# Undivided exponentials, parameter loads on another queue, an earlier end of the first half, and split operands for every second layer

## The reference

```python
# x (512, 64, 768), H = 4 heads, E = 8 experts, HD = 384
scores  = where(x.sum(-1) != 0, x @ aw, -inf)            # (512, 64)
feature = einsum('bl,bld->bd', softmax(scores), x)       # (512, 768)
g       = softmax(relu(feature @ gW1[h] + gb1[h]) @ gW2[h] + gb2[h])   # per head h
gate    = g[row, D[row]]                                 # (512, 8)
h1 = relu(BN1(feature @ eW1[e] + eb1[e]))                # per expert: (512, 768)
h2 = relu(BN2(h1 @ eW2[e] + eb2[e]))                     # per expert: (512, 384)
rep = einsum('be,ebo->bo', gate, h2)
out = softmax((rep @ hW[h] + hb[h])[row, D[row]])        # (512, 2)
```

## Time and profile before

| | |
|---|---|
| median of 3 runs (lowest, highest) | 595.87 us (595.14, 596.85) |
| the profiled execution | 595.4 us, span 593.6 us |
| PE busy | 514.3 us (87%) |
| DVE busy | 482.8 us (81%) |
| ACT busy | 454.4 us (77%) |
| moved | 168.05 MB, mean 283 GB/s |

### The profile page before, as it was taken

How to read it: one execution, slowest core, us unless ns; L and a number is a source line. 1 busy time by engine, 2 the same in 40 slices (tenths; PEclk the granted TensorE clock), 3 DMA queues, 4 the chain that set the end, 5 groups by cost and what they waited for, 6 DMA issues and landing times.

```text
span 593.6 us, 11283 instructions
## 1 busy us (share of the span) xinstructions
PE 514.3 (87%) x4191; PEld 416.1 (70%) x4191; DVE 482.8 (81%) x961; ACT 454.4 (77%) x1007; POOL 81.2 (14%) x118
## 2 busy tenths in 40 slices
PE   0456576666899999999999999899999999999995
PEld 0111121211878888878888888789999999999995
DVE  6989999998799898888999999765376767566753
ACT  5989999997699989888899899564555655565651
POOL 0000000001022030211212121111222222222200
PEclk9976777867799999999999999999999999999998
DMA  8999999999999999999889973545555665666520
GB/s 314 400 367 402 400 401 402 385 367 362 402 396 397 381 394 390 381 382 354 311 311 341 362 277 121 161 137 180 168 160 163 192 182 179 181 184 195 164 77 0
DMA packets 52339, 168.05 MB, mean 283 GB/s; under 512 B 4797, under 2 KB 5041, under 8 KB 52285
## 3 DMA queue, kind: packets, MB, share of 16 engines
q1 hardware_dynamic: 36012, 100.88, 44.6%
q0 software_dynamic: 16128, 66.07, 33.9%
q10 hardware_dynamic: 144, 0.39, 0.2%
HBM read 167.32 MB, written 0.00 MB: 282 GB/s over the span
## 4 chain that ended last, share of the span: by engine, by line
PE 56%; DVE 22%; DMA 11%; issue 7%; ACT 2%; SPq 1%; ACTq 0%; DVEq 0%
PE z_ps L880 15%; PE z_ps L881 15%; PE z_ps L882 15%; DVE prod_out L631 14%; DMA xring<-in_r_x_dram 11%; PE feat_ps L942 5%; DVE wlo L619 4%; PE z_ps L911 4%; ACT copy_out L434 1%; DVE h_hi L687 1%; DVE h L707 1%; PE turn_ps L975 0%; SPq L360 0%; DVE score L631 0%; ACT whi L419 0%
## 5 line engine op out<-in xcount | busy, mean ns | idle before, releaser
L631 DVE CUSTOM_DVE_ANT_0 prod_out<-xring,aw_bc 128x768 bf16<-128x768 f32 x256 | 233.3, 946 | 6.9 <-DMA xring<-in_r_x_dram 6.3
L434 ACT ACTIVATE copy_out<-xring 128x768 bf16<-128x768 f32 x256 | 212.6, 832 | 9.9 <-DMA xring<-in_r_x_dram 8.9
L880 PE MATMUL z_ps<-feat_hi,whi 128*128 128x256 f32 x720 | 207.5, 288 | 2.5 <-DVE feat_lo L666 1.2
L881 PE MATMUL z_ps<-feat_lo,whi 128*128 128x256 f32 x720 | 204.6, 284 | 0.0
L882 PE MATMUL z_ps<-feat_hi,wlo 128*128 128x256 f32 x720 | 204.5, 284 | 0.0
L619 DVE TENSOR_TENSOR wlo<-wraw,whi 128x1152 fp32r<-128x1152 f32 x106 | 143.4, 1353 | 69.8 <-ACT whi L419 69.2
L419 ACT ACTIVATE whi<-wraw 128x1152 fp32r<-128x1152 f32 x106 | 122.8, 1159 | 56.5 <-PE z_ps L882 56.4
L880 PEld LDWEIGHTS z_ps<-feat_hi,whi 128*128 128x128 f32 x720 | 139.2, 193 | 4.0 <-DVE feat_lo L666 1.6
L881 PEld LDWEIGHTS z_ps<-feat_lo,whi 128*128 128x128 f32 x720 | 139.0, 193 | 0.0
L882 PEld LDWEIGHTS z_ps<-feat_hi,wlo 128*128 128x128 f32 x720 | 138.9, 193 | 0.0
L942 PE MATMUL feat_ps<-xring,pwin 128*32 128x384 f32 x1024 | 114.6, 586 | 19.2 <-ACT pwin L452 19.2
(11 more groups left out here) (102 smaller groups left out, 333.8 us busy)
## 6 DMA issues: line engine op xcount, KB each, us to landing
xring<-in_r_x_dram SPq DMA_DIRECT2D x128, 768.0 KB, 8.1
wraw<-in_L_rec_eW_dram POOLq DMA_DIRECT2D x90, 576.0 KB, 4.5
wraw<-in_L_rec_gW_dram POOLq DMA_DIRECT2D x16, 576.0 KB, 4.5
w2raw<-in_L_rec_eW_dram POOLq DMA_DIRECT2D x6, 576.0 KB, 7.4
aw_bc<-in_L_rec_aw_dram ACTq DMA_DIRECT2D x1, 384.0 KB, 5.5
w2raw<-in_L_rec_gW_dram SPq DMA_DIRECT2D x1, 48.0 KB
h<-in_L_rec_eb_dram SPq DMA_DIRECT2D x1, 24.0 KB
h<-in_L_rec_bn_g_dram SPq DMA_DIRECT2D x1, 24.0 KB
```

What stands on the lines that cost most here:

```text
L434: nc.scalar.activation(copy_out[:, t % 2, :], xring[:, r % RING_ROUNDS, j, i, :], ACT.Copy, accum_out=rowsum[:, r % 2, t:t + 1]).then_inc( ...
L631: nc.vector.tensor_tensor_reduce(out=prod_out[:, t % 2, :], in0=xring[:, r % RING_ROUNDS, j, i, :], in1=aw_bc[:, :], scale=1.0, scalar=0.0 ...
L880: nc.tensor.matmul(psum_tile, w_hi, a_hi, start=first, stop=False)
L881: nc.tensor.matmul(psum_tile, w_hi, a_lo, start=False, stop=False)
```

## The change

- The exponentials stay undivided. Four more elements stand behind each row of `xring`, the first of them a one, so the second half of `feat_ps` gets a 385th column, the sum of the exponentials of each row. `copy_rows` takes its reciprocal once per block (`norm`) and scales the rows with it. `softmax_norm` and the sums of `softmax_exp` go. Rows of `xring` are now 772 elements apart and not 768.
- The twelve parameter loads are issued by POOL, after the second score tile, and not by SP.
- At the end of the first half: in the last round ACT takes `softmax_exp` and `place_probs` of the round before earlier, DVE takes `softmax_max` ahead of the parameters, `copy_rows(1)` stands ahead of the tiles of round 16, of which two move behind `features_lo(1)`, and unit 0 waits for the first half of the split features only.
- `NATIVE = 0`: the second layers of experts 0 to 2 of the first half are split like all others, and the panels stand in the order a, c of the expert before, b from the start.
- The stationary operand that picks an expert's gate is read as a broadcast of `sel` and no longer copied by DVE (`pick_gate` goes).

```diff
-NATIVE = 3
+NATIVE = 0
...
-        xring = sb("xring", [P, RING_ROUNDS, CG, 2, DM])
+        xring = sb("xring", [P, RING_ROUNDS, CG, 2, DM + 4])
+        x_in = xring[:, :, :, :, 0:DM]
...
-            for r in range(RING_ROUNDS, ROUNDS):
+            for r in range(ROUNDS):
                 load_round(r)
...
+            pool.wait_ge(zeroed, 1)
+            pool.wait_ge(scored, 2)
...
+                pool.dma_start(prm_rows[at:at + src.shape[0], a, :], src).then_inc(prm_loaded, 16)
...
             for r in range(FIRST_ROUNDS):
-                sum_rows(r, range(0, 4))
+
+                at = 3 if r == FIRST_ROUNDS - 1 else 4
+                sum_rows(r, range(0, at))
                 if r:
                     softmax_exp(r - 1)
-                sum_rows(r, range(4, 5))
+                sum_rows(r, range(at, at + 1))
+                if r:
+                    place_probs(r - 1)
+                sum_rows(r, range(at + 1, at + 2))
                 if r == BLOCK_ROUNDS + 1:
                     copy_rows(0)
-                sum_rows(r, range(5, 7))
-                if r:
-                    place_probs(r - 1)
-                sum_rows(r, range(7, ROUND_TILES))
+                sum_rows(r, range(at + 2, ROUND_TILES))
...
             def copy_rows(b):
                 dve.wait_ge(feat_added, (b + 1) * BLOCK_ROUNDS)
-                nc.vector.tensor_copy(rows[:, DM // 2:DM], feat_ps[:, 1, 0:DM // 2]).then_inc(rows_b, 1)
+                if b:
+                    dve.wait_ge(rows_a, b)
+                nc.vector.reciprocal(norm[:, :], feat_ps[:, 1, DM // 2:DM // 2 + 1]).then_inc(norm_ready, 1)
+                dve.wait_ge(norm_ready, b + 1)
+                nc.vector.tensor_scalar(rows[:, DM // 2:DM], feat_ps[:, 1, 0:DM // 2], norm[:, :], None,
+                                        ALU.mult).then_inc(rows_b, 1)
...
-                if third == 2 and FIRST_ROUNDS < r <= ROUNDS:
-                    softmax_norm(r - 1)
...
-                if s in (gate_at(c) for c in range(NCH)):
-
-                    pe.wait_ge(feat_ready, 2 * CB * (UNITS[s][0] + 1))
+                for c in range(NCH):
+
+                    if s - gate_at(c) in (0, 1):
+                        pe.wait_ge(feat_ready, 2 * CB * (c + 1) - 1 + s - gate_at(c))
                 unit(s)
```

More of the change, by code:

```diff
@@ L133, in rec_kernel @@
         ADD_SLOT = {unit_of(c, "c", q, 1) + 2: (c, q) for c in range(NCH) for q in range(E) if (c, q) != (NCH - 1, E - 1)}
-        PICK_SLOT = {unit_of(c, "c", q, 0): (c, q) for c in range(NCH) for q in range(E)}
+        GATE_SLOT = {unit_of(c, "c", q, 1): (c, q) for c in range(NCH) for q in range(E)}
         def gate_at(c):
@@ L196, in rec_kernel @@
         head_is = sb("head_is", [P, NBLK, H])
-        sel = sb("sel", [P, E])
-        pick = sb("pick", [P, P], F32R)
+        sel = sb("sel", [P, E], F32R)
         gl = sb("gl", [P, CB, E])
@@ L349, in load_round @@
                     b, rb = divmod(r, BLOCK_ROUNDS)
-                    sp.dma_start(xring[:, r % RING_ROUNDS, j, :, :],
+                    sp.dma_start(x_in[:, r % RING_ROUNDS, j, :, :],
                                  x_v[b, rb, :, j, :, :]).then_inc(x_loaded[r % RING_ROUNDS][j], 16)
[L353 to L366, removed]
-            for r in range(RING_ROUNDS, ROUNDS):
+            for r in range(ROUNDS):
                 load_round(r)
@@ L433, in sum_rows @@
                         act.wait_ge(mask_ready, r - 1)
-                    nc.scalar.activation(copy_out[:, t % 2, :], xring[:, r % RING_ROUNDS, j, i, :], ACT.Copy,
+                    nc.scalar.activation(copy_out[:, t % 2, :], x_in[:, r % RING_ROUNDS, j, i, :], ACT.Copy,
                                          accum_out=rowsum[:, r % 2, t:t + 1]).then_inc(summed, 1)
@@ L455, in copy_rows @@
             def copy_rows(b):
-                act.wait_ge(feat_added, (b + 1) * BLOCK_ROUNDS)
-                nc.scalar.activation(rows[:, 0:DM // 2], feat_ps[:, 0, 0:DM // 2], ACT.Copy).then_inc(rows_a, 1)
+                act.wait_ge(norm_ready, b + 1)
+                nc.scalar.activation(rows[:, 0:DM // 2], feat_ps[:, 0, 0:DM // 2], ACT.Copy,
+                                     scale=norm[:, :]).then_inc(rows_a, 1)
             def features_hi(b, g):
@@ L808, in _ @@
                     mask_scores(r - 1)
-                score_tiles(r, range(1, 3))
+                score_tiles(r, range(1, 2))
                 if r:
                     softmax_max(r - 1)
+                score_tiles(r, range(2, 3))
                 if r == BLOCK_ROUNDS + 2:
@@ L936, in add_features @@
                 for i in range(2):
-                    if i and between is not None:
-                        turn_scores(between)
                     at = WIN - (4 * in_block + 2 * i)
                     for half in range(2):
+                        if between is not None and (i, half) == turn_at:
+                            turn_scores(between)
                         for j in range(CG):
-                            last = nc.tensor.matmul(feat_ps[32 * j:32 * j + 32, half, 0:DM // 2],
+                            last = nc.tensor.matmul(feat_ps[32 * j:32 * j + 32, half, 0:DM // 2 + half],
                                                     pwin[:, 2 * j + i, at:at + 32],
-                                                    xring[:, r % RING_ROUNDS, j, i, DM // 2 * half:DM // 2 * (half + 1)],
+                                                    xring[:, r % RING_ROUNDS, j, i,
+                                                          DM // 2 * half:DM // 2 * (half + 1) + half],
                                                     start=(in_block == 0 and i == 0),
@@ L965, in gate_broadcast @@
                     pe.wait_ge(gated_ready, n)
-                nc.tensor.matmul(gate_bc, pick[:, :], gateT[:, :], start=True, stop=True).then_inc(gate_bc_ready, 1)
+                nc.tensor.matmul(gate_bc, sel[:, q:q + 1].to_broadcast([P, P]), gateT[:, :], start=True, stop=True).then_inc(gate_bc_ready, 1)
             def gate_logits(c):
```

68 lines of the change are left out of this document (31 added, 37 removed).

## The result

The changed kernel takes 588.87 us (median of 4 runs, 588.21 to 589.30) against 595.5 before (a fourth run beside the three of the table ahead): ratio 0.9886, 95% interval 0.9864 to 0.9908. Forecast were 589.2 us and "faster". Its profiled execution took 588.99 us, its span is 587.2.

A forecast was written before the change was run, and what follows sets the result against it. It took the stream of x to bound the first half, DVE beside PE the split slots. First-half gains of 5.6 us and the panels' effect gave 6.2 in all: 595.4 - 6.2 = 589.2 us, own range 586.5 to 592.

The forecast's parts named there:

- What bounds it: The stream of x paces the first half, DVE nearly as much as PE the split slots, PE alone the end.
- PE waits for `wlo` or `h1` in slots 20 to 50: A sign in the second half that would show the forecast right: PE waiting there for these DVE outputs.
- (a): First half, parameter loads moved off SP: the gap in the stream of x closes, 0.7 us, bounds 0 and 1.4.
- (b): First half, no division on DVE: it is some 0.2 us behind at the last load, not 1.4; gain 1.2 us.
- (c): Last round of the first half, probabilities placed earlier: mask to products 4.3 us, not 5.4; gain 1.1, bounds 0 and 2.4.
- (d): End of the first half, from round 15's products to the first unit: 2.9 us after them, not 5.5; gain 2.6.
- part 1: The first half: four gains sum to 5.6 us, first unit at about 146.1, bounds 148.8 and 143.4.
- Full DMA takes 1.4 of it: Round 16's last loads come through a full DMA, so DVE starts 4.2 us earlier, not 5.6.
- Part 2: Unsplit panels and second half: PE alone gains 5.5 us, DVE gets net 9.4 more; total gain 4.9 to 8.5, taken 6.2.
- DVE keeps up: Rival: DVE's idle time shrinks further or it starts as early as PE; gain 11.1, 584.3 us; chance 0.13.
- DVE takes nearly all: Rival: about 9 us of DVE's idle time stay, PE gains only some 2.4 us, 593.0 us; chance 0.20.
- The longer pitch: Rival: rows of x 3,088 bytes apart slow the stream; at 5% the time is 598.5 us; chance 0.08.

The follow-up runs named there:

- experiment 10: Changed kernel with the gating of experts 3, 4 and 5 of the first half cut to 2 of 256 columns: 587.03 us, one run.
- experiment 5: Changed kernel with the twelve parameter loads back in SP's queue between rounds 3 and 4: 589.82 us.
- experiment 0: The changed kernel run again, unedited, as the measure for the others: 588.68 us.
- Experiment 6: Changed kernel with the scores of round 9 turned after the first quarter of the products, not the third: 588.79 us.
- Experiment 4: Changed kernel with copy_rows(1) behind the three tiles of round 16 again and unit 0 waiting for both halves of the split features: 591.11 us.
- experiment 2: Kernel before the change with only NATIVE = 0, so all panels split and divisions kept: 598.94 us.
- experiment 1: Changed kernel with NATIVE = 3, the second layers of experts 0 to 2 kept in fp32: 587.40 us.
- 7b: Changed kernel with NATIVE = 1, one panel left unsplit: 587.47 us.

## Why the prediction was right, step by step

The forecast 589.2 us lies 0.3 us from the measured 588.9. What bounds the kernel was right; that the sum came so near is in part luck, as its parts were off both ways.

- **What bounds it**: right. DVE's busy time (209.6; 209.5 forecast), its idle rest (3.9 us; 4.3 forecast) and the length of its stretch came as worked out, and experiment 10 shows directly, for units 29 to 51, that DVE sets the pace. The way it does so was not foreseen: the sign "PE waits for `wlo` or `h1` in slots 20 to 50" did not come. All of PE's 5.5 us of waits between 170 and 375 us are for ACT's `h`, and ACT stands at DVE's maxima for 9.7.
- **(a)** 0.7: some 0.5 (experiment 5).
- **(b)** is the step that failed: "Without it DVE is faster than the stream and no longer 136.23 - 134.86 = 1.4 us behind at the last load, but some 0.2". Counted from the landing of that load, DVE was 1.7 us behind before the change and 1.4 after it (135.43 against 134.04), 1.9 in experiment 0. An edit that the list of the change leaves out turns the scores of the next round after the third quarter of the products and not after the second; I had not followed it through round 10. There DVE stood 2.3 us and was 3.6 behind in round 11, and it regains only 0.35 to 0.55 us a round. Experiment 6 undid this alone, and the lag was gone, but the time stayed: these 1.2 us were not worth anything at the end.
- **(c)** 1.1, or 2.4 if the clock is up: mask to products took 2.9 us (137.19 to 140.09) instead of 5.4, a gain of 2.5, with the clock up. In experiment 0, at the lower clock, it was 1.0.
- **(d)** 2.6: 5.8 us (140.09 to 145.86) instead of 8.3, a gain of 2.6; 2.2 in experiment 0. Experiment 4 puts 2.4 us on the whole time.
- **The sum of part 1** was 5.6 and came as 5.8 in the profiled pair, with (b) nearly at nothing and (c) at its bound. That is luck of the executions: in experiment 0 the same code gives 3.2, and over all traces with either code the first unit is 1.8 to 5.9 us earlier. From the bounds that the prediction gives for (a) and (c) follow 147.9 and 144.1 for the first unit, not 148.8 and 143.4.
- **Full DMA takes 1.4 of it**: 1.6 of the lead was gone at unit 6, but not by the loads alone. Left out was the gain of the first units at the higher clock (2.0 us by unit 2, where the prediction had up to 2.3); PE then lost 3.7 us, most of it to its waits for ACT and to the lower clock behind them. A DVE start 4.2 us earlier was forecast; the first tile of round 17 was 5.0 earlier.
- **Part 2**: the gain "between 4.9 and 8.5" was 6.4 at unit 51 in experiment 0 (6.5 in the first profile), where I took 6.2. DVE handed on 6.0. That it hands on only what it starts earlier is not borne out: in experiment 0 it starts 1.8 us later than in the first profile and ends its stretch only 0.1 later, with 2.6 us idle instead of 3.9. What the parts are worth I had not seen either. PE's 3.4 us on panels, which stand in "PE alone would gain 5.5", are no gain by themselves: alone the split is a loss of 3.8 (experiment 2), here of 1.6 from unit 6 to 51. The division, which I counted as relief of DVE and a stall of 2.06, is worth 3.8 where panels stay unsplit and 7.5 where they don't. For these executions 4.2 from the first half, 3.8 from the division, less 1.6 for the split make the 6.4.
- **Rivals**: *DVE keeps up* fell here; with two panels unsplit and one wait less it is nearly so, 585.8. *DVE takes nearly all* fell as DVE began earlier and kept 3.9 us idle, not 9. *The longer pitch* fell: 402 GB/s.

Two things stay open. Between executions of the same code the start of unit 6 differs by up to 3.7 us; in the first profile and in experiment 1 a lower clock between 162 and 170 us (0.79, where it is 1.00 in experiments 0 and 7b) is part of it. And no kernel that computes the whole result goes below 94.5 us in units 29 to 51, 1.3 above experiment 10: DVE's work there has not been moved elsewhere.

## What to carry to other kernels

Where two engines are both near full, compare their idle times in that stretch before trading work between them: here DVE had 14.6 us idle in 80 with all three panels unsplit and 0.6 with all three split, and the time was lowest in between (two of three unsplit, though one and three can't be told from it). Undo each part alone before calling it a gain, since one part can pay for another. When a transpose or another small step is moved within a queue, follow the one round in which something else stands ahead of it.

## What the runs showed of the hardware

Rows of x that lie 3,088 and not 3,072 bytes apart cost the stream nothing: 402 GB/s in both. The clock granted to PE in the thin part at the end of the first half differed between executions of one program, 0.88 and 0.64 from 134 to 147 us. With the lower one the first unit came 2.6 us later, 1.3 of them in one batch of products (2.79 us instead of 1.51). By unit 6 nothing of this was left in these two executions, as the one that was ahead lost it to a longer wait and to a lower clock between 162 and 170 us.
